# Where the sum over the pixels is kept, and which engine divides it

## The reference, cut to what matters

```python
q  = _ln(reduce_feats, ln_q_w, ln_q_b) @ Wq.T          # one query per patch
kv = _ln(unf, ln_kv_w, ln_kv_b) @ Wkv.T                # one key, one value per pixel, n = 16 pixels
attn   = jax.nn.softmax(jnp.einsum('bhpd,bhpnd->bhpn', q * scale, k), axis=-1)
aggre  = jnp.einsum('bhpn,bhpnd->bhpd', attn, v)       # the sum over the 16 pixels
return reduce_feats + aggre @ proj_w.T + proj_b
```

## Time and profile before

| what | value |
|---|---|
| median of 3 runs | 2413.96 us (2413.16 to 2414.79) |
| the profiled execution | 2413.36 us, span 2411.6 us |
| busy, share of the span: PE, DVE, ACT, POOL | 93%, 78%, 73%, 78% |
| granted TensorE clock, mean | 0.986 |
| first stage | to about 2000 us of the span |

### The profile page before, as it was taken

One profiled execution on the slowest core, in us unless ns is written; L12 is line 12 of the kernel. 1 busy time (PEld: TensorE's weight loads), 2 busy tenths in 40 slices (PEclk: granted clock), 3 DMA queues, 4 the chain that ended last, 5 costly groups with the idle time before them and its releaser, 6 DMA issues. The chain is left out here.

```text
span 2411.6 us, 89169 instructions
## 1 busy us (share of the span) xinstructions
PE 2253.4 (93%) x31921; PEld 1015.0 (42%) x31921; DVE 1882.0 (78%) x4131; ACT 1772.0 (73%) x4281; POOL 1885.6 (78%) x2077
## 2 busy tenths in 40 slices
PE   0799999999999999999999999999999977999997
PEld 0344444444444444444444444444444442222222
DVE  5588888888788888888888888888888867777775
ACT  0888888888888888888888888888888734555554
POOL 3599999999999999999999999999999741333333
PEclk9999999999999999999999999999999978999999
DMA  4333333333333333333333333333333100100001
GB/s 84 72 72 72 73 78 76 76 73 72 72 72 72 72 72 72 74 77 76 76 72 72 72 71 72 72 72 72 74 78 76 25 1 5 23 22 22 22 22 27
DMA packets 573777, 147.82 MB, mean 61 GB/s; under 512 B 573504, under 2 KB 573504, under 8 KB 573504
## 3 DMA queue, kind: packets, MB, share of 16 engines
q1 hardware_dynamic: 573504, 143.53, 29.9%
HBM read 135.10 MB, written 8.39 MB: 59 GB/s over the span
## 5 line engine op out<-in xcount | busy, mean ns | idle before, releaser
L600 ACT ACTIVATE xd<-xb 128x512 f32<-128x512 f32 x512 | 586.1, 1178 | 0.0
L885 DVE TENSOR_TENSOR kqs<-ps,qqT 128x512 f32<-128x512 f32 x512 | 352.8, 689 | 286.5 <-PE ps L394 280.0
L389 PE MATMUL ps<-xd,w_ckv 64*64 64x512 f32 x2048 | 551.6, 615 | 7.5 <-ACT sqs L582 5.5
L394 PE MATMUL ps<-xd,w_ckv 64*64 64x512 f32 x2048 | 551.6, 615 | 0.0
L714 POOL TENSOR_TENSOR pv<-vs,aw 128x512 f32<-128x512 f32 x512 | 534.8, 1077 | 0.0
L582 ACT ACTIVATE sqs<-ps 128x512 f32<-128x512 f32 x512 | 307.6, 601 | 196.3 <-PE ps L394 196.2
L772 POOL TENSOR_TENSOR xt<-xb 128x512 f32<-128x512 f32 x256 | 323.5, 1289 | 58.0 <-DMA xb<-in_x_dram 35.1
L896 DVE TENSOR_TENSOR sm<-ps,decay 128x1024 f32<-128x1024 f32 x256 | 301.3, 1219 | 28.7 <-PE ps L473 24.8
L724 POOL TENSOR_TENSOR pv<-pv 128x512 f32<-128x512 f32 x256 | 322.2, 1283 | 0.0
L416 PE MATMUL ps<-w_ckv,xd 64*64 64x64 f32 x16384 | 297.9, 221 | 0.0
L416 PEld LDWEIGHTS ps<-w_ckv,xd 64*64 64x64 f32 x16384 | 263.5, 135 | 49.5 <-issue 34.4
(11 more groups left out here) (225 smaller groups left out, 3910.3 us busy)
## 6 DMA issues: line engine op xcount, KB each, us to landing
xb<-in_x_dram SPq DMA_DIRECT2D x512, 256.0 KB, 4.3
out_dram<-outb SPq DMA_DIRECT2D x128, 64.0 KB, 1.6
w1p<-in_L_ffn_w_dram SPq DMA_DIRECT2D x16, 16.0 KB
w2p<-in_L_ffn_w_dram SPq DMA_DIRECT2D x8, 16.0 KB
b1p<-in_L_ffn_b_dram SPq DMA_DIRECT2D x8, 0.2 KB
b2v<-in_L_ffn_b_dram SPq DMA_DIRECT2D x8, 2.0 KB
sm<-in_L_tok_Wkv_dram SPq DMA_DIRECT2D x4, 16.0 KB, 2.1
w_av<-in_L_attn_w_qkv_dram SPq DMA_DIRECT2D x4, 16.0 KB, 2.2
```

Source lines behind the costliest of these rows:

```text
L389: nc.tensor.matmul(KB[own, :], w_ckv[own, 2 * P + m * C:2 * P + (m + 1) * C], xd[own, j, :], start=True, stop=True)
L394: mm = nc.tensor.matmul(CB[(1 - m) * C:(2 - m) * C, :], w_ckv[own, m * C:(m + 1) * C], xd[own, j, :], start=True, stop=True)
L600: nc.scalar.activation(xd[:, j, :].rearrange("p (b t) -> p b t", b=ST), xb[:, f, :].rearrange("p (b t d) -> p d b t", b=ST, d=ST)[:, j], A ...
L885: V.tensor_tensor(kqs[:, j, :].rearrange("p (b t) -> p b t", b=ST), KB.rearrange("p (b t) -> p b t", b=ST), qqT[:, s, :].unsqueeze(1).to_b ...
```

## The change

The tile `agg` in SBUF goes. VectorE's sum over the pixels (L909) now writes columns 24 to 31 of `sgr`, in PSUM bank 4. Since the transpose ahead of it writes the same bank, the sum waits for the transpose's semaphore (`turn_done`) where it waited for GpSimd's `agg_done` of the step before. The division moves from GpSimd's queue (ahead of `weighted`) to VectorE's, between `keys(0)` and `keys(1)`. ScalarE, which writes into bank 4 at L647, gets a further wait for `agg_done`.

```diff
-            agg = sb1("agg", [P, P])
@@ ScalarE, ahead of the chain that starts at L647
                     act.wait_ge(turn_done, done(i, r, 1, 1))
+                    act.wait_ge(agg_done, done(i, q, 2, 1))
                     act.wait_ge(den_done, done(i, r, 2, 1))
@@ GpSimd
-                    def normalised():
-                        if there(i, q, 2):
-                            pool.wait_ge(agg_ch, done(i, q, 2, 1))
-                            pool.wait_ge(agT_pe, done(i, q, 3, 1))
-                            nc.gpsimd.tensor_tensor(aggn[:].rearrange("p (j d) -> p j d", d=D),
-                                                    agg[:].rearrange("p (j d) -> p j d", d=D),
-                                                    rden[:, 1 - s, :].unsqueeze(2).to_broadcast([P, SL, D]),
-                                                    ALU.mult).then_inc(agg_done, 1)
...
                     attention()
-                    normalised()
                     weighted()
@@ VectorE
                         dve.wait_ge(pv_done, done(i, q, 2, 2))
-                        dve.wait_ge(agg_done, done(i, q, 3, 1))
-                        V.tensor_reduce(agg[:], pv[:, 0:8 * P].rearrange("p (n c) -> p c n", c=P), AX,
-                                        ALU.add).then_inc(agg_ch, 1)
+                        dve.wait_ge(turn_done, done(i, r, 1, 1))
+                        V.tensor_reduce(sgr[:, :, TG - D:TG], pv[:, 0:8 * P].rearrange("p (n j d) -> p j d n", j=SL, d=D),
+                                        AX, ALU.add).then_inc(agg_ch, 1)
                     keys(0)
+                    if there(i, q, 2):
+                        dve.wait_ge(agg_ch, done(i, q, 2, 1))
+                        dve.wait_ge(agT_pe, done(i, q, 3, 1))
+                        V.tensor_tensor(aggn[:].rearrange("p (j d) -> p j d", d=D), sgr[:, :, TG - D:TG],
+                                        rden[:, 1 - s, :].unsqueeze(2).to_broadcast([P, SL, D]),
+                                        ALU.mult).then_inc(agg_done, 1)
                     keys(1)
```

## The result

| | before | after |
|---|---|---|
| median | 2414.37 us (2413.16 to 2414.79) | 2445.16 us (2444.43 to 2445.70) |
| profiled execution, span | 2413.36, 2411.6 us | 2444.43, 2442.2 us |

Four executions of each; after to before 1.0128, with a 95% interval of 1.0111 to 1.0146: 30.8 us slower. The forecast was 2431 with a range of 2414 to 2446. The direction is right; the loss is 1.8 times what was forecast, and the time lies 0.8 us inside the upper end of the range.

What follows compares the result with a forecast made beforehand. The chain through the end of VectorE's keys(0), which releases TensorE, was taken as the bound. Per step 0.13 (wait) + 0.01 (PSUM write) = 0.14 us, times 125 = 17.5, on 2413.36: 2430.9, median 2431; range 2414 to 2446.

Steps and rivals of the forecast that it cites:

- the branch forecast: Main case: the sum's wait and PSUM write lengthen each step by 0.14 us, giving 2424 to 2438 us; chance 0.63.
- the rival with ScalarE late: L647's wait for the division delays keys(2) by 0.1 us a step, 12.5 us more, 2444; chance 0.12.
- The bound: In every step the end of VectorE's keys(0) sets when TensorE goes on; work ahead of it is paid in full.
- The sum waits for the transpose: On VectorE, the sum starts 0.77 us after the transpose's start in place of 0.64: 0.13 later each step.
- The row of L976 (0.21): VectorE's start 0.21 us behind the end where further waits follow; upper bound for the sum's delay, 0.30.
- The sum writes PSUM: VectorE's sum writing PSUM in place of SBUF takes 0.01 us more a step, from 0 to 0.04.
- The division on VectorE, and off GpSimd: 0.21 us net in VectorE's idle time behind keys(0), cost 0; 0.41 us a step freed on GpSimd, gain 0.
- ScalarE's wait: At L647 for agg_done: starts 0.53 us behind keys(0), limit 0.59, so cost 0, up to about 0.1.
- The added wait costs nothing: On VectorE, the sum's wait for the transpose is free and only the PSUM write stays: 2415 us; chance 0.14.
- A shorter sum: VectorE's sum shortens when written to PSUM; ScalarE's room limits the gain to 0.05 us a step, 2407; chance 0.09.
- GpSimd was the bound: GpSimd's 0.41 us less decides: at most 34 us gained over 125 steps, 2380 us; chance 0.02.

Runs made afterwards that it cites:

- the neighbouring kernels (2490 and 2467 us): The changed kernel with the sum written to SBUF again, 2490.34 us; the changed kernel with keys(0) ahead of the sum, 2467.16 us.

## Why the prediction was right, and where its size was off

The direction and the path were right. That the number fell inside the range is in part luck: the branch forecast, 2424 to 2438 with a wait of 0.09 to 0.19, missed on both counts, and the range reached to 2446 only for the rival with ScalarE late at 2444, which isn't what happened in the steps that were counted.

- **The bound: right.** What is put between the masks and the end of `keys(0)` was paid in full, and what is put behind it was free: 44 us against 0 for the same division. TensorE's seventh load stayed 0.07 behind its end (0.071 in the mean).
- **The sum waits for the transpose: right mechanism, mis-sized.** Forecast 0.13 a step; it measured 0.195. The end-to-start gap was taken from L943 and L944 as 0.04; it is 0.103. That row holds for an instruction that carries the wait, and where the sum carries this one it is 0.034. "`turn_done` is the last wait before the instruction" was the step that failed: it is the last in the source, but the sum carries the other wait and `turn_done` stands in an instruction of its own. The 0.07 between is worth 8.6 us of the span, shown by moving the other wait. The row of L976 (0.21), taken as the upper bound, held.
- **The sum writes PSUM: +0.01 forecast, +0.007 measured** on the start of `keys(0)` against the same kernel with the sum in SBUF. But a sum with the wait takes 0.03 to 0.04 longer, also into SBUF, and in the kernel after `keys(0)` starts 0.028 later behind it, of which 0.021 is left with the sum in SBUF. That cost of the wait wasn't in the forecast at all; why the sum takes longer stays open. Together 0.223 where 0.14 was forecast: 10.4 us of the 13.1 us by which 30.6 exceeds 17.5.
- **The last steps: left out.** The 125 steps with keys were counted; the 2.7 us of the last two, where ScalarE's wait is late, weren't. How much of it is that wait's was not isolated: with the wait for the transpose alone, and none on ScalarE, the same two steps are 1.2 longer.
- **The division on VectorE, and off GpSimd: 0 and 0, right** as a sum, by the run with the division alone. The 0.284 was right only because the operand is in PSUM: the row used had one too, and the SBUF form takes 0.878 beside GpSimd.
- **ScalarE's wait: 0, right,** with more room than counted. L647 starts 0.244 behind the end of the division, for which four waits in full made 0.32; that is 0.441 behind `keys(0)` and not 0.53, and L650 ends 0.065 ahead of `centred(1)`. At the overlap of 0.095 seen where they are bound, that is 0.16 of room, not 0.06.
- **The rivals.** "The added wait costs nothing" falls: neighbours without a wait overlap by 0.09, with one they stand 0.034 to 0.13 apart. The rule on the pipeline flush that the Trainium skill gives ("VectorE: DVE Perf Modes", section "The DRAIN you can't avoid"), that a semaphore costs nothing extra, was measured there on eight copies and doesn't hold for this pair. "A shorter sum" falls: the write to PSUM took nothing off the 1.94. "GpSimd was the bound" falls: taking its 0.41 away, at the price of 0.87 in VectorE's idle time, gave 0.9999. "ScalarE late" is real in the neighbouring kernels (2490 and 2467 us) and not in this one, except in the last steps.

## What to carry to other kernels

Find the instruction whose end releases the engine that is the bound, and price an edit by which side of that instruction it stands on; busy shares say nothing of it. A wait of one VectorE instruction for the one ahead of it costs even though the two run in that order anyway: the overlap at the ends goes, and where the instruction has a second wait, the one that comes last may not be the one it carries. Look in the trace, step by step, which one it is; a mean over steps can hide two cases. Move a wait that is long over to an earlier instruction that has slack, not to one that is itself waited for. When a new operand goes to SBUF, look at what GpSimd does at that moment.

## What the runs showed of the hardware

- VectorE, start of an instruction against the end of the one before it: -0.09 us without a wait, +0.034 with one that it carries, +0.10 with one in a wait instruction ahead of it, +0.12 to +0.13 with one in a register instruction ahead of it. For this pair: 0.640, 0.766, 0.835 and 0.853 to 0.862 us from start to start. Where the wait instruction had two semaphores it was 0.864.
- A 128x128 product on VectorE with both operands in SBUF took 0.878 us when it started beside GpSimd's products and 0.292 when it started with GpSimd idle; with one in PSUM 0.284 beside the same products. The Trainium skill has the rule ("SBUF — State Buffer", section "Who interferes with whom"): such an instruction and one of GpSimd that reads SBUF contend, since its second input comes through the read interface that the two engines share. The trace agrees, in both directions: beside VectorE's three additions GpSimd's own went from 0.42 to 0.87 us.
- A reduction that reads SBUF 512 bytes apart took the same, within 0.014 us, written to PSUM or SBUF: 1.979 against 1.965 and 1.975 behind the wait, and 1.94 in both where it had no transpose to wait for.
